# Expert tiles of a mixture-of-experts layer: the next tile's rows turned in mid-step, stores one step later, a full-height last contraction tile

## What is computed

```python
logits = jnp.einsum('th,eh->te', xf, w_router)
probs = jax.nn.softmax(logits, axis=-1)
topw, topi = jax.lax.top_k(probs, TOP_K)
topw = topw / jnp.sum(topw, axis=-1, keepdims=True)
...
gate = jax.nn.silu(jnp.einsum('th,eih->eti', xf, w_gate))
up = jnp.einsum('th,eih->eti', xf, w_up)
down = jnp.einsum('eti,ehi->eth', gate * up, w_down)
out = jnp.einsum('eth,te->th', down, combine)
```

## Time and profile before

| | us |
|---|---|
| runs (three) | 2282.08, 2282.25, 2285.61; median 2282.25 |
| the profiled execution's span | 2282.2 |
| PE busy | 1917.5 (84%) |
| DVE busy | 1104.6 (48%) |
| ACT busy | 953.2 (42%) |
| POOL busy | 263.3 (12%) |

### The profile page before, as it was taken

One profiled execution on the slowest core, in us unless ns is written; L12 is line 12 of the kernel. 1 busy time (PEld: TensorE's weight loads), 2 busy tenths in 40 slices (PEclk: granted clock), 3 DMA queues, 4 the chain that ended last, 5 costly groups with the idle time before them and its releaser, 6 DMA issues.

```text
span 2282.2 us, 31517 instructions
## 1 busy us (share of the span) xinstructions
PE 1917.5 (84%) x9728; PEld 822.9 (36%) x9729; DVE 1104.6 (48%) x1481; ACT 953.2 (42%) x1663; POOL 263.3 (12%) x215
## 2 busy tenths in 40 slices
PE   6799969999799675859999999999998449999980
PEld 2334423333244232323333333333332336666650
DVE  4662258775211415348777677677761301111115
ACT  3331237667311424324676577567676102112220
POOL 5042010000200203110000000000001230000005
PEclk9899979999899797968999999999999569999995
DMA  9011141001000003250000000000001710000003
GB/s 334 22 41 34 15 102 29 27 28 38 23 0 0 5 0 45 31 124 8 9 15 9 9 16 8 9 9 15 1 2 41 302 59 27 28 28 28 28 25 110
DMA packets 64104, 96.04 MB, mean 42 GB/s; under 512 B 11504, under 2 KB 56752, under 8 KB 62074
## 3 DMA queue, kind: packets, MB, share of 16 engines
q1 hardware_dynamic: 60922, 86.21, 13.1%
q0 software_dynamic: 3072, 8.39, 1.2%
HBM read 65.20 MB, written 28.97 MB: 41 GB/s over the span
## 4 chain that ended last, share of the span: by engine, by line
PE 56%; issue 7%; DVE 4%; ACT 2%; POOL 2%; DMA 1%; SPq 1%; DVEq 0%; ACTq 0%; POOLq 0%
PE ps L1159 10%; PE ps L1117 9%; PE ps L517 9%; PE ps L1807 8%; PE ps L1183 8%; PE ps L1822 5%; PE ps L1464 2%; DVE arena L1316 2%; PE ps L441 1%; PE ps L1218 1%; POOL arena L1921 1%; PE ps L1815 1%; DMA qparts<-arena 1%; ACT arena L1875 1%; PE ps L1801 1%
## 5 line engine op out<-in xcount | busy, mean ns | idle before, releaser
L1265 ACT ACTIVATE arena<-ps 128x512 f32<-128x512 f32 x1088 | 596.3, 598 | 281.1 <-PE ps L1183 280.7
L1316 DVE TENSOR_REDUCE arena<-ps 128x1 f32<-128x802 f32 (+1 forms) x512 | 498.0, 990 | 144.4 <-PE ps L1117 135.0
L517 PE MATMUL ps<-arena 128*128 (+1 forms) x832 | 383.2, 621 | 73.5 <-DVE arena L1605 23.2
L1117 PE MATMUL ps<-arena 97*128 97x401 bf16 (+2 forms) x1280 | 351.9, 358 | 47.4 <-DVE arena L1316 18.8
L1183 PE MATMUL ps<-arena 100*128 100x512 bf16 x1088 | 374.6, 386 | 5.4 <-issue 4.8
L1159 PE MATMUL ps<-arena 128*32 128x256 f32 x4352 | 348.9, 393 | 0.6 <-ACT arena L1265 0.3
L517 PEld LDWEIGHTS ps<-arena 128*128 128x128 f32 x832 | 164.1, 199 | 291.6 <-issue 291.6
L1807 PE MATMUL ps<-arena 128*128 x608 | 198.9, 470 | 29.2 <-ACT arena L1875 29.2
L1117 PEld LDWEIGHTS ps<-arena 97*128 97x128 bf16 x1280 | 96.1, 99 | 252.3 <-issue 123.5
L2002 DVE TENSOR_TENSOR arena<-ps,arena 128x352 f32<-128x352 f32 x76 | 40.0, 526 | 269.6 <-ACT arena L1882 197.5
L1313 DVE TENSOR_REDUCE arena<-ps 128x2 f32<-128x1024 f32 x128 | 154.5, 1221 | 27.7 <-PE ps L1117 27.2
(11 more groups left out here) (187 smaller groups left out, 1452.1 us busy)
## 6 DMA issues: line engine op xcount, KB each, us to landing
arena<-in_experts_w SPq DMA_DIRECT2D x8, 2176.0 KB, 17.6
arena<-qparts SPq DMA_DIRECT2D x192, 64.0 KB, 2.3
qparts<-arena SPq DMA_DIRECT2D x48, 128.0 KB, 2.0
rows_in<-arena SPq DMA_DIRECT2D x1, 5120.0 KB, 34.4
arena<-in_ctxT SPq DMA_DIRECT2D x3, 1664.0 KB, 8.7
kparts<-arena SPq DMA_DIRECT2D x24, 208.0 KB, 2.4
arena<-kparts SPq DMA_DIRECT2D x12, 416.0 KB, 14.6
arena<-rows_in SPq DMA_DIRECT2D x38, 128.0 KB, 2.1
```

The source lines that it names most:

```text
L517: ins = eng.matmul(out, w[:, k, m * P:(m + 1) * P], x[:, k, tok(c)], start=k == 0, stop=k == ktiles - 1)
L1117: ins = eng.matmul(slot_banks(s_static)[:, x, 0:n_keys], Qst[0:97, ring, heads[x], q * P:(q + 1) * P], Kst[0:97, at_head(ring * HG + heads ...
L1265: eng.activation(probs[:, keys_of(u, kt) % 2, h, :], ring_bank(r), ACT.Exp, bias=0.0).then_inc(ring_read.sem, 1)
L1316: eng.tensor_reduce(MX[:, par, heads[0] * QT + q, n % 2:n % 2 + 1], got, AX.XY, ALU.max).then_inc(slot_free.sem, 1)
```

## The change

In PE's step the two transposes of the next tile's rows come ahead of the second half of gate/up, and no longer behind the down product. In ACT's step the copy of these rows comes ahead of the second half's silu. SP's step stores the tile before last where it stored the last one, so the store stands behind a later load in the queue; one more store follows the last step. The down product's sixth contraction tile is taken over all 128 partitions; the partitions 64 to 127 of its hidden tile are set to zero once, ahead of the router, and the packed weights are zero there already.

```diff
             def step(j, u, last):
                 if not last:
                     load(j + 1, 1 - u)
-                if not first(j):
-                    store(j - 1, 1 - u)
+                if not early(j):
+                    store(j - 2, u)

             final = run_tiles(eng, step)
+            store(final - 1, 0)
             store(final, 1)
...
             def down_product(expert):
                 for i in range(FT):
-                    m = min(P, FE - i * P)
-                    ins = eng.matmul(ps[:, 7, 0:D], hiddenT[0:m, i, :],
-                                     experts_all[0:m, bass.ds(expert * EW + (4 * FE + i * D), D)],
+                    ins = eng.matmul(ps[:, 7, 0:D], hiddenT[:, i, :],
+                                     experts_all[:, bass.ds(expert * EW + (4 * FE + i * D), D)],
                                      start=i == 0, stop=i == FT - 1)
...
                     turn_hidden(1 - u)
+                if not last:
+                    turn_rows(j + 1, 1 - u)
                 gate_up(expert, u, 1)
                 if not first(j):
                     finish(j - 1, last_expert)
-                if not last:
-                    turn_rows(j + 1, 1 - u)
...
                     copy_hidden(j - 1)
-                silu_half(j, 1)
                 if not last:
                     copy_rows(j + 1, 1 - u)
+                silu_half(j, 1)
...
             norm4.wait_all(eng)
+            eng.memset(hiddenT[FE - 5 * P:P, 5, :], 0.0)
             eng.wait_ge(lg_mm, 1)
```

## The result

Before 2282.35 us (median of four runs, 2282.08 to 2285.61), with the change 2228.78 us (four runs, 2224.70 to 2232.03): ratio 0.9756, 95% interval 0.9743 to 0.977. The ratio is the comparison's own figure; the two medians alone give 2228.78 / 2282.35 = 0.9765. The profiled execution of the changed kernel took 2230.99 us and has a span of 2229.0 us; the time of an execution is some 2 us more than its span.

A forecast was written before the change was run, and what follows sets the result against it. PE bounds the kernel, with about 28 us idle in the expert stage. Savings of 49.4 + 0.7 + 0.3 + 0.2 = 50.6 us from 2282.2 give 2231.6 us; range 2227 to 2243.5.

The forecast's parts named there:

- The mechanism and its price: Expert stage: PE's idle row-copy hand-over and late 64-row weight loads vanish, 1.37 us saved a step, 49.4 over 36.
- The step: One expert-stage step on PE: 4.74 + 0.65 + 0.22 + 2.60 = 8.21 us, against 9.58.
- the bounds for the transposes: Moved row transposes: 0.16 us with two weight loads overlapped, 0.54 with old 0.38 plus a late load; 0.22 taken.
- The edges: Border of tiles 0 and 1, at lower clock, saves 0.66 us; last tile's step saves 0.29 and 0.2.
- The covers: Copies, register loads and row loads finish before PE needs them: 1.5 us spare at down, 1.6 at ACT's silu.
- The split: Of 1.37 us saved a step: row copy and hand-overs 0.98, 64 rows 0.29, slow first pass 0.10.
- The slow first pass of gate/up: First gate/up half took 2.47 us instead of 2.37 because it started after PE's idle spell; 0.10 a step.
- The rule on weight loads and row groups: Weight loads overlap matmuls in flight only in different row groups; padding the down product's last tile would then gain nothing.
- rival A: Down product: the 64 rows don't cause the long distances; step 8.50 us, time 2242.5; chance 5%.
- Rival D: Expert stage: eight transposes in one run drop the clock to 1.2 GHz, 8.2 us a step, up to 2527; 2%.
- How the numbers follow: Closing step for the whole kernel's time: forecast 86%, bounds 2229.4 and 2243.1, range 2227 to 2243.5, faster 0.96.
- the bounds of the step: Row transposes at 0.16 or 0.54 us instead of 0.22, over 36 steps, give 2229.4 or 2243.1 us.

The follow-up runs named there:

- e3: Changed kernel with the down product's last contraction tile back at 64 rows and no memset, so the new order alone: 2247.59 us, ratio 0.9838 against the kernel before.
- e4: Kernel before with only the memset and the down product's last contraction tile over 128 rows, order unchanged: 2270.03 us, ratio 0.9937.

## Why the prediction was right, and where it was wrong

The mechanism and its price were right. Point by point:

- The step: 8.21 us forecast, 8.21 measured. Gate/up 2.37 a half, row transposes 0.22 in their new place, down product 2.60. The value chosen between the bounds for the transposes (0.16 to 0.54) was the right one.
- The edges and the sum: 50.6 us forecast, 50.8 measured in the stage. The steps make 49.4 of them, so the edges gave 1.4 where 1.2 was forecast; the first tile's lower clock did not change the picture.
- The covers held: in the loop no wait of PE is left, and with the store put back the one that it was to prevent appeared.
- The split was slightly off. The new order alone gave the 0.98 us a step that the row copy and its hand-overs were priced at (9.58 to 8.60); the 64 rows gave 0.39 in the new order and 0.34 in the old one, not 0.29. The slow first pass of gate/up (0.10) was given to the idle spell; e3 shows it behind 64 rows without an idle spell, and e4, where an idle spell is left but no 64 rows, keeps the first half of gate/up at the old 2.47. Either of the two is enough. The sum was not touched, since the change removes both.
- The rule on weight loads and row groups that the prediction cites from the Trainium skill's page "TensorE: Matmul & The Clock Gate", Part 3, section "The mechanism", would have led to rival A's 2242.5. The trace does not agree with it: the full-row load of 2007.77 starts one pass ahead of its own pass of 2007.98.
- Rival D: the clock stayed at 1.00 with eight transposes in a row.

What failed is the step "How the numbers follow", at the lower end of the range: the sum gave the part of the kernel outside the expert stage no term of its own, as if it stood still from one execution to the next. The ratio of 0.9756 puts the changed kernel at 0.9756 × 2282.25 = 2226.6 us on the base of the prediction, and the range ended at 2227.0; the median of 2228.78 lies inside it. I built that end from the bounds of the step (2229.4) and left 2.4 us below it for the runs, although the three runs shown were 3.5 us apart (the prediction says 3.4). The 2229.4 itself rests on 0.16 us for the row transposes, a bound that stands beside no row of the trace; they cost 0.22.

In its place the runs showed a stage that gave the forecast gain, 50.8 us, and a part outside it that moved by 2.4 us more in the first profile, and by 3 between two executions of one program. It goes with the clock: of the 14 runs of the changed kernel the two shortest, 2224.70 and 2226.57 us, are both in the first comparison and have the highest mean granted clock, 0.927 and 0.926; the two longest, 2235.82 and 2234.43, have 0.920 and 0.919. So the first ratio was low in part by chance: the later two, 0.9768 and 0.9783, give 2229.3 and 2232.7 on the same base, inside the range. With 3 us for that part the end would have been 2229.4 − 3 = 2226.4, just low enough. A second slip went the other way: I set the profiled execution's span equal to the median of the runs, while a time is some 2 us more than its span (2230.99 against 2229.0), so that execution took about 2284 us and was slower than the median of 2282.25 shown; from the 61 runs' median of 2283.38 the same sum gives 2232.8. Of the three comparisons of the changed kernel the forecast of 2231.6 lies 2.8 above, 1.1 above and 0.7 below the median.

## What to carry to other kernels

When the bound engine's idle time ends on a short chain through another engine (transpose, copy, matmul), move the start of that chain to where the bound engine still has independent work, and then check the queue that feeds it: here a store one place earlier in SP's list would have taken back 23.6 of 50.8 us. A last contraction tile of 64 rows was dearer here than a full one; padded with zeros it saved 0.34 us a step in the old order and 0.39 in the new one. The distances of the passes around it gave most of that price, 0.29; the first pass behind it has to be counted too. And give the parts of the kernel that a change doesn't touch a term for their own wander, measured as the spread of the runs, before choosing the ends of a range.

## What the runs showed that I had not expected

A 64-row tile costs more than its own passes show: behind it the next product's load comes late too (0.30 us to its start, where full rows take 0.22), and that product's own first pass is long (0.40 us instead of 0.30). And the clock ahead of the stage, with the same program and the same data, was 0.83 in one execution and 0.89 in another over the same 60 us, with PE busy 46.35 and 45.50 us in them. Over the 14 profiles the stage started anywhere from 1850.3 to 1854.1 us, while each kernel's stage kept its length within 0.2 us.
